# Two raw buffers for the weights, loaded two pairs ahead, and another opening, in a fused attention and network kernel

## The reference, cut to what matters

```python
xn = layernorm(x)
Q, K, V = xn @ Wq + bq, xn @ Wk + bk, xn @ Wv + bv      # 512 x 1024 weights, 16 heads of 64
scores = einsum('bhid,bhjd->bhij', Q, K)
columns = where(abs(j - i) <= 64, scores, 0.0)           # a band; outside it the score is 0
out = softmax(columns) @ V @ Wo + bo                     # softmax over all 1024 columns
s = xn @ Win + bin_                                      # 64 wide
g = einsum('btmh,mh->btm', relu(s[..., None] * W1 + b1), W2) + b2
x = x + out + g @ Wout + bout
```

## Time and profile before

| | |
|---|---|
| median of 3 runs | 2233.77 us (2233.75 to 2234.09) |
| the profiled execution | 2233.51 us, of which the trace's span is 2231.8 us |
| TensorE busy | 2154.3 us, 97% of the span |
| VectorE busy | 1832.5 us, 82% |
| ScalarE busy | 1514.3 us, 68% |
| GpSimd busy | 917.0 us, 41% |
| mean DMA rate | 51 GB/s |

### The profile page before, as it was taken

How to read it: one execution, slowest core, us unless ns; L and a number is a source line. 1 busy time by engine, 2 the same in 40 slices (tenths; PEclk the granted TensorE clock), 3 DMA queues, 4 the chain that set the end, 5 groups by cost and what they waited for, 6 DMA issues and landing times.

```text
span 2231.8 us, 45652 instructions
## 1 busy us (share of the span) xinstructions
PE 2154.3 (97%) x16263; PEld 1310.0 (59%) x16263; DVE 1832.5 (82%) x5062; ACT 1514.3 (68%) x4217; POOL 917.0 (41%) x1313
## 2 busy tenths in 40 slices
PE   6879899999999999999999999999999999999998
PEld 4445565656655666565665666656565666665664
DVE  4667787888788888888888888798878888888877
ACT  4666676777667667676667666676767767667665
POOL 3756644533253342533244343353334334253323
PEclk8889999999999999999999999999999999999999
DMA  3121211301112110221112111031111211021111
GB/s 102 58 85 39 77 35 33 114 29 34 34 48 88 37 39 24 73 76 30 30 30 85 59 39 29 30 109 34 30 38 48 86 39 38 22 76 30 34 34 48
DMA packets 69760, 112.94 MB, mean 51 GB/s; under 512 B 6664, under 2 KB 18976, under 8 KB 69536
## 3 DMA queue, kind: packets, MB, share of 16 engines
q1 hardware_dynamic: 69488, 110.02, 15.7%
q10 hardware_dynamic: 48, 0.01, 0.0%
HBM read 84.84 MB, written 25.17 MB: 49 GB/s over the span
## 4 chain that ended last, share of the span: by engine, by line
PE 82%; DVE 10%; POOL 2%; ACT 2%; DMA 1%; issue 1%; SPq 1%; DVEq 0%; ACTq 0%; POOLq 0%
PE ps L1183 38%; PE ps L1198 13%; PE ps L1236 9%; PE ps L1169 8%; PE ps L1249 8%; PE ps L1226 3%; DVE acc L880 2%; DVE pT_lo L927 2%; DVE probs L852 2%; DMA w_raw<-in_L_attn_Wk 1%; PE ps L1109 1%; PE ps L1220 1%; PE ps L1208 1%; DVE xn L898 1%; DVE v_mean L932 1%
## 5 line engine op out<-in xcount | busy, mean ns | idle before, releaser
L1183 PE MATMUL ps<-xT_hi,w_split 128*128 128x512 f16 x3072 | 986.2, 382 | 17.4 <-POOL w_split L336 15.8
L371 POOL TENSOR_SCALAR probs<-probs,inv_l,neg_e 128x256 f32<-128x256 f32 x1024 | 568.6, 572 | 815.7 <-DVE neg_e L871 815.7
L495 ACT ACTIVATE probs<-probs,neg_max 128x256 f32<-128x256 f32 x1024 | 506.2, 497 | 154.7 <-DVE neg_max L859 154.4
L1183 PE MATMUL ps<-xT_lo,w_split 128*128 128x512 f16 x1536 | 586.8, 382 | 0.0
L1183 PEld LDWEIGHTS ps<-xT_hi,w_split 128*128 128x128 f16 x3072 | 302.7, 99 | 364.0 <-issue 24.3
L852 DVE CUSTOM_DVE_ANT_0 probs<-ps,mask,unit_s 128x256 f32<-128x256 f32 x1024 | 433.7, 480 | 59.6 <-PE ps L1169 56.1
L880 DVE SCALAR_TENSOR_TENSOR acc<-ps,unit_o,acc 128x512 f32<-128x512 f32 x512 | 370.9, 743 | 86.8 <-PE ps L1198 85.7
L550 ACT ACTIVATE pT_hi<-ps 128x512 f16<-128x512 f32 x512 | 276.2, 597 | 189.9 <-PE ps L1249 166.6
L927 DVE TENSOR_TENSOR pT_lo<-ps,pT_hi 128x512 f16<-128x512 f32 x512 | 322.2, 682 | 16.3 <-ACT pT_hi L550 16.1
L1198 PE MATMUL ps<-wo_split,oT_hi 128*128 128x512 f16 x1024 | 309.6, 384 | 11.3 <-DVE top_used L758 4.1
L378 POOL TENSOR_TENSOR oT_lo<-o_sum,oT_hi 128x512 f16<-128x512 f32 x128 | 148.6, 1161 | 410.7 <-ACT o_sum L563 410.7
(11 more groups left out here) (123 smaller groups left out, 2925.3 us busy)
## 6 DMA issues: line engine op xcount, KB each, us to landing
w_split<-w_kept SPq DMA_DIRECT2D x168, 256.0 KB, 2.6
acc<-in_L_attn_x SPq DMA_DIRECT2D x14, 1024.0 KB, 6.8
out_x<-acc SPq DMA_DIRECT2D x14, 1024.0 KB, 4.6
wo_split<-wo_kept SPq DMA_DIRECT2D x56, 256.0 KB, 2.7
w_kept<-w_split SPq DMA_DIRECT2D x24, 256.0 KB, 4.7
acc<-in_L_attn_x SPq DMA_DIRECT2D x4, 512.0 KB, 5.3
w_raw<-in_L_attn_Wv SPq DMA_DIRECT2D x8, 256.0 KB, 5.1
w_raw<-in_L_attn_Wq SPq DMA_DIRECT2D x8, 256.0 KB, 5.5
```

Of the source, the lines that this page charges most:

```text
L371: pool.tensor_scalar(probs[:, h, t], probs[:, h, t], inv_l[:, c:c + 1], neg_e[:, c:c + 1], ALU.mult, ALU.add).then_inc(normed, 1)
L495: act.activation(probs[:, h, t], probs[:, h, t], ACT.Exp, bias=neg_max[:, c:c + 1], accum_out=row_sum[:, c:c + 1])
L1183: last = pe.matmul(dst[:], w[wp][:, i, c], xT[xp][:, c, half * LINE:half * LINE + LINE], start=(c == 0 and a == 0), stop=(c == KC - 1 and ...
```

## The change

- `w_raw` and `wo_raw` have two buffers each, one for even and one for odd pairs, with semaphores of their own. Pair 1's three weights and Wo's first rows are loaded in the opening; from then on step k loads the three weights of pair k+2 behind their predecessor's store, and the output rows of pair k+1.
- In the opening the raw Wq and Wk are loaded ahead of the third and fourth quarter of x. The three scales of pair 0 go through one chain: one pair of matmuls, one read, one root, one power of two. The statistics of the first half of x go ahead of the squares of the biases on VectorE. The high half of Wv stands ahead of Win's square on ScalarE, that of Wq ahead of three of the four copies of x, that of Wk ahead of the second half's normalising. On GpSimd the low half of Wq goes ahead of the root for the second half of x, and the mask is cleared last.

```diff
-        w_raw = sb("w_raw", [P, 3, KC, P])
+        w_raw = sb("w_raw", [P, 2, 3, KC, P])
-        wo_raw = sb("wo_raw", [P, E])
+        wo_raw = sb("wo_raw", [P, 2, E])
...
-                sp.dma_start(w_raw[:, i], w_d[i][pair]).then_inc(w_in[i], 16)
+                sp.dma_start(w_raw[:, pair % 2, i], w_d[i][pair]).then_inc(w_in[i][pair % 2], 16)
...
-            def load_output_raw(pair, splits):
-                if splits > 0:
-                    sp.wait_ge(wo_lo, splits)
-                sp.dma_start(wo_raw[:], wo_d[pair]).then_inc(wo_in, 16)
+            def load_output_raw(pair):
+                if pair > 1:
+                    sp.wait_ge(wo_lo, pair - 1)
+                sp.dma_start(wo_raw[:, pair % 2], wo_d[pair]).then_inc(wo_in[pair % 2], 16)
...
                 if i == 1:
-                    load_raw(V_, 0)
-            load_raw(Q_, 0)
-            load_raw(K_, 0)
+                    for m in (V_, Q_, K_):
+                        load_raw(m, 0)
...
+            for i in (V_, Q_, K_):
+                load_raw(i, 1)
+            load_output_raw(0)
...
                         keep_weights(n, i, k)
-                        if split_next:
-                            load_raw(i, k + 1)
+                        if k < PAIRS - 2:
+                            load_raw(i, k + 2)
...
-                    load_output_raw(k, n)
+                    if split_next:
+                        load_output_raw(k + 1)
...
             inverse_deviation(slice(0, 4), 1)
-            inverse_root(slice(0, 1), top_ready, 1, root_ready)
+            inverse_root(slice(0, 3), top_ready, 1, root_ready)
             split_low(0, V_)
-            inverse_root(slice(1, 3), top_ready, 2, root_ready)
+            split_low(0, Q_)
+            inverse_deviation(slice(4, T), 2)
+            split_low(0, K_)
+            inverse_root(slice(4, 5), win_top_ready, 1, win_root_ready)
             pool.memset(mask[:], 1.0).then_inc(pool_set, 1)
-            inverse_deviation(slice(4, T), 2)
-            inverse_root(slice(4, 5), win_top_ready, 1, win_root_ready)
-            split_low(0, Q_)
-            split_low(0, K_)
...
             for t in (0, 1):
                 normalise(0, t)
+            split_high(0, V_)
             act.wait_ge(win_in, 16)
...
             x_high(0, 0)
-            split_high(0, V_)
+            split_high(0, Q_)
             for i in range(1, 4):
                 x_high(0, i)
-            split_high(0, Q_)
+            split_high(0, K_)
             for t in (4, 5):
                 normalise(0, t)
-            split_high(0, K_)
...
+            read_tops(slice(0, 3), FIRST_TOP_BANK[0], top_sum, 1, top_ready)
             statistics(0, 4)
+            dve.wait_ge(root_ready, 1)
+            power_of_two(slice(0, 3), w_scale[:, 0, 0:3], top_split, w_scaled, 1)
...
-            pe.wait_ge(w_top[V_], 1)
-            sum_tops(slice(0, 1), FIRST_TOP_BANK[0], 0, top_sum)
+            for i in (V_, Q_, K_):
+                pe.wait_ge(w_top[i], 1)
+            sum_tops(slice(0, 3), FIRST_TOP_BANK[0], 0, top_sum)
```

More of the change, by code:

```diff
@@ L111, in band_attention_ffn @@
         BIAS_BANK = 1
-        TOP_BANK, FIRST_TOP_BANK, TOP_COLUMN = 3, (1, 3, 6), 32
+        TOP_BANK, FIRST_TOP_BANK, TOP_COLUMN = 3, (1, 6), 32
         WARM_UP = 28
@@ L119, in band_attention_ffn @@
         x_in = [sem(f"x_in_{i}") for i in range(2)]
-        wo_in = sem("wo_in")
-        w_in = [sem(f"w_in_{s}") for s in "vqk"]
+        wo_in = [sem(f"wo_in_{s}") for s in range(2)]
+        w_in = [[sem(f"w_in_{s}{p}") for p in range(2)] for s in "vqk"]
         w_got, wo_got = [sem(f"w_got_{s}") for s in "vqk"], sem("wo_got")
@@ L164, in f32, with scales_of @@
             return a.bitcast(F32)
-        def scales_of(pair, i):
-            return 1 if pair == 0 and i == V_ else 2 + pair
+        def scales_of(pair):
+            return pair + 1
         def output_scales_of(pair):
-            return 4 + pair
+            return pair + 3
         def scaled_in(step):
-            return step + 3
+            return step + 2
         def tops_of_step(n):
@@ L428, in weights_top @@
             def weights_top(n, i):
-                act.wait_ge(w_in[i], 16 * (n + 1))
+                act.wait_ge(w_in[i][n % 2], 16 * (n // 2 + 1))
                 if n > 0:
-                    act.wait_ge(top_sum, scales_of(n - 1, K_))
-                act.activation(squares[:, i], w_raw[:, i].rearrange("p k c -> p (k c)"), ACT.Square,
+                    act.wait_ge(top_sum, scales_of(n - 1))
+                act.activation(squares[:, i], w_raw[:, n % 2, i].rearrange("p k c -> p (k c)"), ACT.Square,
                                accum_out=top[:, i:i + 1]).then_inc(w_top[i], 1)
             def output_top(pair):
-                act.wait_ge(wo_in, 16 * (pair + 1))
+                act.wait_ge(wo_in[pair % 2], 16 * (pair // 2 + 1))
                 if pair > 0:
                     act.wait_ge(top_sum, output_scales_of(pair - 1))
-                act.activation(squares[:, 3], wo_raw[:], ACT.Square, accum_out=top[:, 3:4]).then_inc(w_top[3], 1)
+                act.activation(squares[:, 3], wo_raw[:, pair % 2], ACT.Square, accum_out=top[:, 3:4]).then_inc(w_top[3], 1)
             def split_high(n, i):
-                act.wait_ge(w_scaled, scales_of(n, i))
+                act.wait_ge(w_scaled, scales_of(n))
                 if n > 0:
@@ L446, in split_high @@
                     act.wait_ge(w_got[i], 16 * n)
-                act.activation(w[hi][:, i], w_raw[:, i], ACT.Identity, scale=w_scale[:, n, i:i + 1]).then_inc(w_hi, 1)
+                act.activation(w[hi][:, i], w_raw[:, n % 2, i], ACT.Identity, scale=w_scale[:, n, i:i + 1]).then_inc(w_hi, 1)
             def normalise(b, t):
@@ L704, in step @@
                         act.wait_ge(wo_got, 16 * j)
-                    act.activation(wo[hi][:], wo_raw[:], ACT.Identity, scale=w_scale[:, j + 2, 3:4]).then_inc(wo_hi, 1)
+                    act.activation(wo[hi][:], wo_raw[:, j % 2], ACT.Identity, scale=w_scale[:, j + 2, 3:4]).then_inc(wo_hi, 1)
                 if n == 0:
@@ L785, in biases_and_unit @@
             def biases_and_unit(pair):
-                dve.wait_ge(w_scaled, scales_of(pair, K_))
+                dve.wait_ge(w_scaled, scales_of(pair))
                 dve.tensor_tensor(bias_scaled[:, :, pair], bias_qkv[:, :, pair, 0], w_scale[:, pair, 0:3], ALU.mult) \
@@ L792, in biases_and_unit @@
                 dve.reciprocal(unit_s[:, pair:pair + 1], unit_part[:, 0:1]).then_inc(unit_s_ready, 1)
+            for t in tiles_of(0):
+                statistics(0, t)
+            mean_and_variance(tiles_of(0), 4, 1)
             dve.wait_ge(bias_in, 2)
@@ L798, in _ @@
                                      bias_qkv[:, Q_:, :, 0], ALU.mult, ALU.mult).then_inc(bias_squares, 1)
-            for t in tiles_of(0):
-                statistics(0, t)
-            mean_and_variance(tiles_of(0), 4, 1)
-            read_tops(slice(0, 1), FIRST_TOP_BANK[0], top_sum, 1, top_ready)
             shift_rows(slice(0, 4), 1)
-            dve.wait_ge(root_ready, 1)
-            power_of_two(slice(0, 1), w_scale[:, 0, 0:1], top_split, w_scaled, 1)
             first_rows(2)
             first_rows(3)
+            read_tops(slice(0, 3), FIRST_TOP_BANK[0], top_sum, 1, top_ready)
             statistics(0, 4)
+            dve.wait_ge(root_ready, 1)
+            power_of_two(slice(0, 3), w_scale[:, 0, 0:3], top_split, w_scaled, 1)
             x_low(0, 0)
@@ L1149, in _ @@
                         last.then_inc(xT_done, 1)
-            pe.wait_ge(w_top[Q_], 1)
-            pe.wait_ge(w_top[K_], 1)
-            sum_tops(slice(1, 3), FIRST_TOP_BANK[1], 0, top_sum)
             pe.wait_ge(w_top[4], 1)
-            pe.matmul(ps[FIRST_TOP_BANK[2]][:, TOP_COLUMN + 4:TOP_COLUMN + 5], ones[:], top[:, 4:5], start=True, stop=True) \
+            pe.matmul(ps[FIRST_TOP_BANK[1]][:, TOP_COLUMN + 4:TOP_COLUMN + 5], ones[:], top[:, 4:5], start=True, stop=True) \
                 .then_inc(win_top_sum, 1)
```

13 lines of the change are left out of this document (5 added, 8 removed).

## The result

| | before | changed |
|---|---|---|
| median of 4 runs | 2233.93 us (2233.75 to 2234.37) | 2200.34 us (2197.47 to 2200.92) |
| ratio, 95% interval | 1 | 0.9847 (0.983 to 0.9864) |
| profiled execution | 2233.51 us, span 2231.8 | 2200.26 us, span 2198.5 |
| TensorE busy | 2154.3 us | 2139.7 us |

The change saves 33.6 us; 34.3 were forecast, which gave a median of 2199.5 us. In the trace of the changed kernel step 1 starts at 55.53 us, step 2 at 92.24, step 7 at 267.48 and step 8 at 303.15 (before 58.41, 98.19, 300.74 and 336.40).

A forecast was written before the change was run, and what follows sets the result against it. TensorE bounds quiet steps; the first batch loses time to late raw loads and the half clock after each stall. 21.75 + 5.5 + 2.7 + 4.3 = 34.3 us off gave 2199.5 us, range 2190 to 2210 (8 in 10).

The forecast's parts named there:

- The main term: Steps 2 to 6, up to the second V projection: raw loads in time, VectorE's order binds next; 21.75 us saved.
- (c): Rival: loads no sooner, SyncE still holding them behind a waiting store; only opening and order count, 2229 us; chance 0.03.
- The tail: Steps 2 to 6, second V projection to step end: half the slow-clock time comes back, 5.5 us, bounds 0 to 5.5.
- Step 1: Step 1: ScalarE's wait for raw Wk goes, and half clock behind TensorE's stall may go; 2.7 us, bounds 0 to 2.9.
- The opening: Up to step 0's first Q projection: x's second half normalised sooner, Q projection at 24.1; 4.3 us, bounds 1.0 to 5.0.
- (a): Rival: TensorE alone bounds the first batch's steps, VectorE being in time; 12 us more saved, 2187.5 us; chance 0.08.
- (b): Rival: short stalls in steps 2 to 6 keep the clock low, 2.6 us each, 13 in all; 2207 to 2213; chance 0.15.
- (d): Rival: slower, remaining stalls hold half clock for the rest of the step; with all five about 2294 us; chance 0.03.

The follow-up runs named there:

- e5_read_first: The changed kernel with VectorE's read of the sums (top_used) moved ahead of the low half of the first Q in steps 1 to 7: 2196.51 us.
- e2_opening_only: The changed kernel with single raw buffers and the old times of the loads, so only the new opening stays: 2229.26 us.
- e9_changed_again: The changed kernel, unaltered, measured a second time on another chip: 2202.77 us.
- the loads alone: The kernel before with only the two raw buffers and the loads two pairs ahead, its opening kept: 2207.83 us.
- e4_queue_order: The kernel before, single buffers, with SyncE's store of split output weights and load of Wo's next rows behind the next step's Wq store and load: 2210.36 us.

## Why the prediction was right

**The main term, 21.75 us: right, and the next bound was the one forecast.** From the start of the step to the second V projection steps 2 to 6 took 22.73, 22.28, 19.12, 17.21 and 21.40 us before and 17.15, 16.23, 15.32, 15.61 and 16.61 now (V projections at 109.39, 144.67, 178.48, 213.32 and 247.83): 21.8 saved. The stall went, VectorE's order was late next, and e5_read_first showed that by moving it. What the term needs is that the loads are in time, not that there are two buffers (see (c) below). The waits for `top_used` were 1.05, 0.98, 0.64, 1.02 and 0.85 us, somewhat under the 1 to 1.5 forecast; the place was right, since it was worked from neg_max's end and not from the wait.

**The tail, 5.5 us: right in size.** From the V projection to the end of the step 0.65, 0.16, 1.73, 1.41 and 1.54 us were saved, 5.5 in all. The fear that VectorE's `pT_lo` would take it did not come true; TensorE's waits for it are 1.07, 0.49 and 1.20 in steps 2 to 4, as they had been.

**Step 1, 2.7 us: 3.1.** The wait of 2.47 for `pT_lo` at 88.22 fell to 0.47, but those for the splits were 5.6 in place of 4.1; half clock shrank from 12.6 to 9.6 us. The term is right to 0.4; its parts were not. Some of it is where half clock falls: e2_opening_only had this step in 38.23 us with single buffers.

**The opening, 4.3 us: 2.9 in this execution, the step that was mis-sized, and 4.8 in the next.** Its own milestones held: V's high split began at 12.07 (12.0 forecast), the V projection at 15.76 (15.7), the normalising of the second half at 20.08 (20.4), the Q projection at 23.57 (24.1). But I let the Q projection last as before, and it did not: before it ran at full clock, with the V projection at half; now it is the other way round.

```profile
15.76:18.96 3.20, 2.83 (x12) 1.00 0.97 220
23.57:28.12 4.55, 4.55 (x13) 0.56 0.64 213
```

Before, the Q projection took 2.58 us and the V projection 5.10. A V projection that is 2 us faster is worth nothing there, since x's second half ends last; a Q projection that is 2 us slower is on the path. In the second trace of the same kernel (e9_changed_again) the V projection is mostly at half clock and the Q projection at full:

```profile
16.25:20.67 4.42, 4.42 (x12) 0.58 0.85 231
23.31:25.90 2.59, 2.59 (x15) 1.00 1.07 352
```

There step 1 started at 53.58, 4.8 us sooner than before; in e2_opening_only, also with a fast Q projection, at 53.19. The forecast lies between the two traces of one program. That the total came out within 0.8 us of it is therefore partly luck: the sum has no term for which projection meets the half clock, 2 us, nor for the half clock behind short stalls, up to 5 us.

**The rivals.** (a), TensorE alone, did not come: VectorE's order stands before it, and the one instruction moved out of the way in e5_read_first gave 0.7 us a step. (b) came in part. In the first trace no short stall was punished; in the second two were, and in the loads alone three, 1.7 us each where I had put 2.6 on each of five steps, and in steps 4 to 6 no trace with loads in time has it. That is a spread of up to 5 us and not the 13 that I gave it. The Trainium skill (TensorE: Matmul & The Clock Gate, section "What's actually happening") says that the gate's watch runs freely and isn't reset when a kernel starts, so that the same work meets it at another place from run to run. The two traces of one program, with the same stalls (0.68 and 0.66 us, 2.85 and 2.86) and other clocks behind them, agree. (c) and (d) did not come. The idea behind (c), though, that the queue and not the buffer is what matters, turned out to be most of the cause: e4_queue_order has 24.0 of the 26.5 us of the loads with single buffers.

## What to carry to other kernels

A load that is late because it stands behind a store that waits is mended first by the order of the queue; the second buffer then bought at most 2.5 us here (2210.4 to 2207.8, not clear of the noise), about what one late load of Wo in step 6 costs in the trace (2.8). To size a stall that goes, work forward from the next engine's own instructions to the next start that counts, rather than add up the stall: here that gave the length of each step to 0.1 us. And a stall of TensorE of 0.7 to 3 us cost here nothing or 1.7 us more, from one execution to the next, so compare kernels by medians of several runs, and look at the clock of a trace before explaining 2 us of difference.

## What the runs showed that I had not expected

The same stall of 2.86 us in the same program was followed by full clock once and by 3.4 us of half clock another time. Adding matmuls that nobody reads made a kernel faster: 92 of them by 9.8 us in the kernel before; 18 of them by 4.0 in the changed one, of which 3.4 are seen as half clock that is gone. And the clock of the first projections differs between two executions of the same program: V fast and Q slow in the first trace of the changed kernel (4.55 us for Q), V slow and Q fast in the second (2.59).
